# Latent attention: the query products of two tiles in one product, half of a pair's blocks in each tile's step, rows turned four tiles ahead

## What is computed

```python
def _L1_xattn_ref(hidden_q, kv_c, Wq, w_kc_q, w_kc_kv, W_qr, W_kr, Wo):
    q_hk = (hidden_q @ Wq.T).reshape(b, s, H, K)                # H = 16, K = 128
    q_big = jnp.einsum('bshk,hkq->bshq', q_hk, w_kc_q)          # q = 192
    kv_rope = kv_c * cos[None] + _rotate_half(kv_c) * sin[None]
    q_r = jnp.einsum('bshq,hqr->bhsr', q_big, W_qr)             # r = 64
    k_r = jnp.einsum('bld,hdr->bhlr', kv_rope, W_kr)
    scores = jnp.einsum('bhsr,bhlr->bhsl', q_r, k_r)            # l = 257 keys
    attn = jax.nn.softmax(scores, axis=-1)
    ctx_c = jnp.einsum('bhsl,bld->bhsd', attn, kv_rope)
    ctx_lat = jnp.einsum('bhsd,hkd->bshk', ctx_c, w_kc_kv)
    return ctx_lat.reshape(b, s, H * K) @ Wo.T
x = x + _L1_xattn_ref(_layernorm(x, axis=-1), ctx_512, ...)
```

## Time and profile before

| | |
|---|---|
| median of 3 executions | 1148.84 us (1146.88 to 1154.70) |
| the profiled execution | 1154.21 us, of which the profile's span is 1152.4 us |
| PE matmul busy in the span | 1087.5 us, 94% |
| DVE, ACT, POOL busy | 708.1 us (61%), 452.3 us (39%), 301.6 us (26%) |
| L1648, query products of the changed phase | 512 matmuls, 67.8 us busy |
| L1711, output products of that phase, 256 columns | 240 matmuls, 54.4 us busy |

### The profile page before, as it was taken

One profiled execution on the slowest core, in us unless ns is written; L12 is line 12 of the kernel. 1 busy time (PEld: TensorE's weight loads), 2 busy tenths in 40 slices (PEclk: granted clock), 3 DMA queues, 4 the chain that ended last, 5 costly groups with the idle time before them and its releaser, 6 DMA issues. The chain is left out here.

```text
span 1152.4 us, 32210 instructions
## 1 busy us (share of the span) xinstructions
PE 1087.5 (94%) x12466; PEld 830.2 (72%) x12467; DVE 708.1 (61%) x1806; ACT 452.3 (39%) x1329; POOL 301.6 (26%) x390
## 2 busy tenths in 40 slices
PE   7898999999999999999979999999998799899996
PEld 6676878888778768989756766776766588556664
DVE  6898754554646475646547888888885687422221
ACT  2453443434435222221145555555553565222221
POOL 1701523323131200000001221221214535234442
PEclk9899999999999999999989999999999998799998
DMA  8631211111121119000202323333244633312211
GB/s 266 173 89 36 71 46 49 43 39 55 27 55 27 37 35 253 1 0 0 57 1 70 92 75 78 77 84 76 70 139 145 200 77 100 84 30 35 35 27 11
DMA packets 72655, 82.56 MB, mean 72 GB/s; under 512 B 28942, under 2 KB 57263, under 8 KB 72140
## 3 DMA queue, kind: packets, MB, share of 16 engines
q1 hardware_dynamic: 64284, 62.33, 20.4%
q0 software_dynamic: 8304, 19.32, 6.4%
HBM read 64.91 MB, written 18.53 MB: 72 GB/s over the span
## 5 line engine op out<-in xcount | busy, mean ns | idle before, releaser
L1780 ACT ACTIVATE xattn_exps<-xattn_ps_s,xattn_top 128x256 f32<-128x256 f32 x256 | 117.8, 474 | 84.7 <-DVE xattn_top L1844 84.7
L777 PEld LDWEIGHTS attn_ps_q<-attn_xnT,w_b_q 128*128 128x128 f32 x1024 | 120.0, 194 | 12.6 <-issue 12.6
L777 PE MATMUL attn_ps_q<-attn_xnT,w_b_q 128*128 128x128 f32 x1024 | 124.6, 278 | 0.0
L831 PE MATMUL attn_ps_out<-w_b_o,attn_oT 128*128 128x256 f32 x480 | 106.6, 380 | 2.6 <-DVE all_x L1012 1.5
L831 PEld LDWEIGHTS attn_ps_out<-w_b_o,attn_oT 128*128 128x128 f32 x480 | 90.0, 190 | 16.1 <-DVE all_x L1012 2.4
L885 ACT COPY attn_qT<-attn_ps_q 128x512 f32<-128x512 f32 x64 | 38.1, 595 | 148.7 <-PE attn_ps_q L777 148.7
L1851 DVE STREAM_TRANSPOSE xattn_expsT<-xattn_exps 128x1024 f32<-128x1024 f32 x64 | 79.5, 1242 | 26.4 <-ACT xattn_exps L1780 26.3
L1841 DVE TENSOR_REDUCE xattn_raw_top<-xattn_ps_s 128x4 f32<-128x1024 f32 x64 | 77.3, 1208 | 14.7 <-PE xattn_ps_s L1671 14.2
L1648 PEld LDWEIGHTS xattn_ps_o<-xattn_xnT,all_d_a 128*128 128x128 f32 x512 | 61.9, 198 | 17.9 <-ACT xattn_exps L1780 7.2
L1613 POOL TENSOR_TENSOR xattn_ctxT<-xattn_weighed_sum,xattn_inverse 128x256 f32<-128x256 f32 x60 | 41.9, 730 | 125.3 <-DMA xattn_inverse<-xattn_inverse_rows 125.3
L1671 PE MATMUL xattn_ps_s<-all_c,xattn_qT 64*32 64x256 f32 x2048 | 69.8, 382 | 2.8 <-ACT xattn_exps L1780 2.8
(11 more groups left out here) (361 smaller groups left out, 2214.7 us busy)
## 6 DMA issues: line engine op xcount, KB each, us to landing
all_c<-roped_kT SPq DMA_DIRECT2D x32, 256.0 KB, 3.9
xattn_inverse<-xattn_inverse_rows SPq DMA_DIRECT2D x30, 256.0 KB, 4.0
attn_k_raw<-in_ctx SPq DMA_DIRECT2D x64, 64.0 KB, 1.9
roped_kv<-attn_k_kv SPq DMA_DIRECT2D x16, 256.0 KB, 2.1
roped_kT<-attn_k_turned SPq DMA_DIRECT2D x64, 64.0 KB, 1.7
all_c<-roped_kv SPq DMA_DIRECT2D x16, 256.0 KB, 2.9
moe_gate<-in_f_gate SPq DMA_DIRECT2D x8, 512.0 KB, 8.2
moe_up<-in_f_up POOLq DMA_DIRECT2D x8, 512.0 KB, 5.2
```

Of the source, the lines that this page charges most:

```text
L777: last = nc.tensor.matmul(ps_q[g % 2][:, h * P:(h + 1) * P], wq[:, c, head * DH:(head + 1) * DH], xnT[u][:, c, :], start=(c == 0), stop=(c ...
L831: last = nc.tensor.matmul(bank[:, 0:DIM], of_heads[:, h, :, :].rearrange("p b q -> p (b q)"), wo[:, h, :], start=(h == 0), stop=(h == HEAD ...
L1780: nc.scalar.activation(exps[g % 2][:, nkeys * k:nkeys * (k + 1)], ps_s[g % 2][:, nkeys * k:nkeys * (k + 1)], ACT.Exp, bias=top[u][:, n:n + ...
```

## The change

Before, each tile had its own query products. Now the tiles go in pairs (0 and 1, 2 and 3, ...). `xnT` has two buffers of 2 x 256 columns, `qT` two buffers for a pair each. In step t the products of half of the blocks are made for the pair that comes next: for even t, blocks 0 to 3 of tiles t + 2 and t + 3; for odd t, blocks 4 to 7 of tiles t + 1 and t + 2. A product now moves 256 columns. Rows are turned for tile t + 4 instead of t + 2; tiles 0 and 1 are both turned at the start, tile 1 in a score bank. PE and ACT have loops of four steps.

```diff
-        step(i, i % 2, lambda d: 0 <= i + d < tiles)
+        step(i, i % unroll, lambda d: 0 <= i + d < tiles)
...
-    xnT = sb("xnT", [P, KC, P])
-    qT = [sb(f"qT{u}", [P, TB, pairs, SEQ]) for u in range(2)]
+    xnT = [sb(f"xnT{v}", [P, KC, 2 * P]) for v in range(2)]
+    qT = [sb(f"qT{v}", [P, 2, TB, pairs, SEQ]) for v in range(2)]
...
+    def turn_bank(t):
+        return ps_s[1] if isinstance(t, int) and t == 1 else ps_turn
...
             def step(t, u, live):
-                if live(1):
-                    row_normalised(t + 1)
+                if live(3):
+                    row_normalised(t + 3)
                 if live(-2):
                     normalised(t - 2, u)
 
+            row_normalised(2)
+            row_normalised(3)
...
-            def queries(t, part):
+            def queries(t, w, part):
+                pair, half = (w // 2 + 1) % 2, w % 2
                 if part == 0:
-                    pe.wait_ge(s["xnT_ready"], t + 1)
-                if isinstance(t, int) and t == 1:
+                    pe.wait_ge(s["xnT_ready"], min(t + 4, TILES) if isinstance(t, int) else t + 4)
+                if isinstance(t, int) and t == 0:
                     pe.wait_ge(s["last_ready"], 1)
-                wait_count(pe, s["sum_ready"], TB * (t - 2) + 1 + part)
-                for n in range(4):
-                    m = 4 * part + n
+                wait_count(pe, s["sum_ready"], TB * (t - 1) + 1 + part)
+                for n in range(2):
+                    m = 4 * half + 2 * part + n
                     for c in range(KC):
-                        last = nc.tensor.matmul(ps_q[part][:, n * P:(n + 1) * P], a_w[:, c, m * P:(m + 1) * P], xnT[:, c, :],
-                                                start=(c == 0), stop=(c == KC - 1))
+                        last = nc.tensor.matmul(ps_q[part][:, n * 2 * P:(n + 1) * 2 * P], a_w[:, c, m * P:(m + 1) * P],
+                                                xnT[pair][:, c, :], start=(c == 0), stop=(c == KC - 1))
...
-            def step(t, u, live):
-                if live(0):
-                    scores(t, u, 0)
+            def step(t, w, live):
+                u = w % 2
+                if isinstance(t, int) and t == -2:
+                    turn(0)
+                    turn(1)
+                if live(0):
+                    scores(t, w, 0)
...
-                if live(1):
-                    queries(t + 1, 0)
-                if live(0):
-                    scores(t, u, 3)
-                if live(1):
-                    queries(t + 1, 1)
+                if live(2):
+                    queries(t, w, 0)
+                if live(0):
+                    scores(t, w, 3)
+                if live(2):
+                    queries(t, w, 1)
...
-                    pe.wait_ge(s["q_out"], 2 * t + 4)
+                    pe.wait_ge(s["q_out"], min(2 * t + 6, 2 * TILES) if isinstance(t, int) else 2 * t + 6)
...
-                if live(2):
-                    turn(t + 2)
-
-            run_steps(pe, step, -2, TILES, 3, TILES - 3)
+                    last_key(t + 1, (w + 1) % 4)
+                if live(4):
+                    if isinstance(t, int) and t == -2:
+                        pe.wait_ge(s["q_out"], 2)
+                    turn(t + 4)
+
+            run_steps(pe, step, -2, TILES, 3, 10, 4)
...
+            def queries_out(t, w, part):
+                pair, half = (w // 2 + 1) % 2, w % 2
+                m = 4 * half + 2 * part
+                act.wait_ge(s["q_made"], 2 * (t + 2) + part + 1)
+                nc.scalar.copy(qT[pair][:, :, :, m:m + 2, :].rearrange("p a b m q -> p m (a b) q"),
+                               ps_q[part][:, :].rearrange("p (m b q) -> p m b q", m=2, q=SEQ)).then_inc(s["q_out"], 1)
...
-            run_steps(act, step, -2, TILES, 2, TILES - 3)
+            run_steps(act, step, -2, TILES, 2, 9, 4)
```

More of the change, by code:

```diff
@@ L83, in run_steps @@
         for k in range(unroll):
-            step(r + k if k else r, (full_from + k) % 2, lambda d: True)
+            step(r + k if k else r, (full_from + k) % unroll, lambda d: True)
     for i in range(full_from + count, last + 1):
@@ L1617, in row_normalised @@
             def row_normalised(t):
-                wait_count(pool, s["turned"], t)
+                pool.wait_ge(s["turned"], t)
                 nc.gpsimd.tensor_scalar(xn[:, :], x_sb[:, t, :], moments.moments[:, t, 0:1], moments.factors[:, t:t + 1],
@@ L1656, in last_key @@
                         last = nc.tensor.matmul(ps_last[odd][SEQ * b:SEQ * b + SEQ, 0:DIM], last_cols[u][rows, b:b + SEQ],
-                                                qT[u][rows, b, :, :].rearrange("p m q -> p (m q)"), start=True, stop=True)
+                                                qT[w // 2][rows, w % 2, b, :, :].rearrange("p m q -> p (m q)"), start=True, stop=True)
                 last.then_inc(s["last_made"], 1)
@@ L1664, in scores_free, with scores @@
                 wait_count(pe, s["exps_ready"], per_group * (groups * t + g - 1))
-            def scores(t, u, g):
+            def scores(t, w, g):
+                u = w % 2
                 for n in range(2):
@@ L1671, in scores @@
                             last = nc.tensor.matmul(ps_s[g % 2][SEQ * b:SEQ * b + SEQ, 512 * odd + nkeys * n:512 * odd + nkeys * (n + 1)],
[L1672 removed]
+                                                    qT[w // 2][rows, w % 2, b, 2 * g + n, :],
                                                     kT[u][rows, b, :], start=True, stop=True)
@@ L1720, in step @@
                         pe.wait_ge(s["last_ready"], t + 1)
-                    if live(1):
-                        pe.wait_ge(s["xnT_ready"], t + 2)
+                    if live(0):
+                        pe.wait_ge(s["xnT_ready"], min(t + 4, TILES) if isinstance(t, int) else t + 4)
                     wait_count(pe, s["x_ready"], t - 1 if live(0) else t - 2)
@@ L1729, in step @@
                 if live(0):
-                    scores(t, u, 1)
+                    scores(t, w, 1)
                 if live(-1):
@@ L1797, in cols_out, with step @@
                 nc.scalar.copy(last_cols[u][:, :], lastT[:, bass.ds(t * TB, TB + SEQ)]).then_inc(s["cols_ready"], 1)
-            def queries_out(t, u, part):
-                act.wait_ge(s["q_made"], 2 * t + part + 1)
-                nc.scalar.copy(qT[u][:, :, 4 * part:4 * part + 4, :].rearrange("p b m q -> p m b q"),
-                               ps_q[part][:, :].rearrange("p (m b q) -> p m b q", m=4, b=TB)).then_inc(s["q_out"], 1)
-            def step(t, u, live):
+            def queries_out(t, w, part):
[4 more added lines that the diff above has]
+                               ps_q[part][:, :].rearrange("p (m b q) -> p m b q", m=2, q=SEQ)).then_inc(s["q_out"], 1)
+            def step(t, w, live):
+                u = w % 2
+                if isinstance(t, int) and t == -2:
+                    turned_out(0, 0)
+                    turned_out(1, 1)
                 if live(0):
```

25 lines of the change are left out of this document (13 added, 12 removed).

## The result

| | before | after |
|---|---|---|
| median of 15 runs each on one chip, us | 1151.43 (1145.36 to 1156.14) | 1163.47 (1156.97 to 1168.83) |
| ratio, 95% interval | | 1.0117 (1.0095 to 1.0138) |
| profiled execution, span, us | 1154.21, 1152.4 | 1166.15, 1164.3 |
| changed phase, first turn to its last product, us | 289.27 | 299.96 |

The account below looks back on a forecast made before the run. PE was taken to bound the kernel; -4.6 (query products) + 5.7 (start) - 0.7 (turns) + 0.8 (step 14) = +1.2 us, which put on the median of 1148.84 gave 1150.0 us, range 1145 to 1156.

Parts of the forecast that it names:

- What bounds the kernel: Whole kernel: PE, with matmuls in 94% of the span, no other engine above 61%.
- (c): Steps 12 and 13: no turns any more, 0.36 us less each, 0.7 us less together.
- (e): Copies of `qT` and loops of four steps instead of two: no change, 0 us.
- (a): Query products in steps 0 to 13: half the passes, twice as wide; 0.33 us less a step, 4.6 us less.
- The rival, to which I gave 0.08: Query products: the removed weight loads were hidden anyway, so the 4.6 us gain falls away; 1154.6 us, chance 0.08.
- my case: Whole kernel: 1147.5 to 1153 us, with the clock kept or lost in step 14; chance 0.59.
- (b): Start of the phase: additional turn, wider passes and a new chain before the first score; 5.7 us more, bounds 5.3 and 7.5.
- (d): Step 14 without query products: new 3.2 us pause and half clock behind it; 0.8 us more, or 0.55 less if clock stays.
- More clock lost, the rival of 0.13: Pause in step 0 or a late clock rise at the start costs more; 1151.5 to 1155 us, chance 0.13.
- the rival of the other side: ACT's copies of `qT` get slow, 1.27 us instead of 0.58; 1% slower, 1160 us, chance 0.05.
- the last line of the prediction: List of signs that would show the forecast wrong, ending with a pause at the loop's end.

Follow-up runs that it names:

- e1: Kernel before with only PE's loop in the phase made four steps long instead of two; median 1156.03 us, ratio 1.0060.
- e2: Changed kernel with PE's steps written out without a loop, ACT keeping its loop of four; median 1163.01 us, ratio 1.0124.
- e6: Kernel before with PE's steps of the phase written out without a loop; median 1155.63 us, ratio 1.0025.
- e8: Changed kernel run again without edits, on another chip than e1 to e4; median 1165.37 us, ratio 1.0101.
- e3: Changed kernel with three idle products in step 14, run in the pause ahead of the output products; median 1158.74 us, ratio 1.0081.
- e4: Changed kernel with each query product of 256 columns cut into two of 128; median 1169.67 us, ratio 1.0175, two runs.
- f2: Kernel before, unchanged, profiled once more; profiled execution 1151.90 us.
- f3: Kernel before, unchanged, profiled once more as a further sample; profiled execution 1147.30 us.
- f4: Kernel before with PE's steps written out, a second trace of e6; profiled execution 1151.80 us.

## Why the prediction was wrong, point by point

- **What bounds the kernel: right for the middle steps.** PE is busy for 16.82 of 17.00 us there and stands still for 0.18 of a step's 16.98, so a step lasts as long as PE's work in it. After the change the 0.18 us ahead of part 0 is still there, and no engine behind PE took the gain. In step 13 one did, see (c).
- **(e) "Loops of four steps instead of two: 0": wrong, and the step that failed.** I read the cost of a jump back off a loop of two steps, and gave it to a body twice as long, which no row showed. The runs showed a pause of 2.7 to 3.2 us in its place: steps 6 and 7 took 4.23 more instead of 0.66 less, e1 shows 0.6% of the kernel from this edit alone, e2 and e6 show that without the jump the pause is gone. It needed a bound of its own. The pauses that the trace did have give an estimate, for the one jump back: 2.9 for the pause and 1.5 for a stretch of 3 us at half clock, some 4.4 us. Measured against two steps without a pause it was 4.5 in the changed kernel and e8, 5.6 in e3, 7.8 and 8.2 in e1 and e4 with their second pauses; so 4.4 was the least of it.
- **(a) Half the passes: right in kind, 4.6 us was 1.5.** I divided the 16-product block's span by 15 and so spread a fixed cost over the passes. A block of the same size in the second phase has none of it:

```profile
219.82 1.95 PE L777 MATMUL attn_ps_q<-attn_xnT,w_b_q 128*128 128x128 f32 x16
```

  This row of before gives (1.95 - 0.275)/15 = 0.112 us a pass. The block of the earlier trace rows is 2.05, so it carries 0.10 once. The starts of its passes in the trace show where: the second comes 0.213 us behind the first, all others 0.112 apart (wide: 0.320, then 0.216). The record of one lasts 0.275 (wide 0.379), so the records overlap, and what a pass costs is the distance of the starts. The block of eight carries it too: (1.99 - 0.10 - 0.379)/7 = 0.216, the very price of the wide output products. By this a part saves 16 x 0.112 - 8 x 0.216 = 0.06 us; measured were 0.06 and 0.05. Twice the columns cost 1.93 times a narrow pass, and 0.112 - 0.216/2 leaves 4 ns for a load, not 10.

  So the removed loads had been hidden up to those 4 ns. Between the rival's 0 and my 4.6, 1.5 was measured. The rival, to which I gave 0.08, was nearer than my case.
- **(b) The start: right in its steps.** 5.7 was forecast. The table's 4.93 is under the lower bound of 5.3, but it sets a low clock before against a high one after; at the same clock it is 5.9 to 6.1. The 0.2 us that the sum takes off for the clock is shown by no run. In its place the runs showed a start that differs from one execution to the next: in the profiled execution before, the clock was 0.50 from the first turn to 593.4, for 6.3 us; in the six profiles with the change (and in f2, f3 and f4) the turn ran at 1.00, and the clock was 0.50 for 3.4 us, from 0.8 to 1.7 us behind the turn on. The chain between the halves was 1.57 (1.65). The additional turn seems to cost 0.70 where I had 1.15, since both turns took 0.44 and not 0.69.
- **(c) The turns: half right.** 0.73 came off the two steps instead of 1.4, and some 0.2 of it is the width's. Step 12 lost 0.63, step 13 only 0.10: there PE meets POOL's `ctxT` (842.95 and 843.00, above) and waits 0.08 us for DVE's last scores. That is the engine behind PE of which (a) gave the 0.59 to spare; with the turn of step 12 gone too, this is used up one step before step 14.
- **(d) Step 14: the mechanism right, the size not.** A pause of 3.34 us (3.2 forecast) with the clock at 0.50 behind it. I weighed the loss at 1.4 from a stretch of 3 us; the clock stayed low for most of the 6.49 us of the output products (0.56 as the mean of 859.2 to 865.7), 2.87 lost. The step cost 2.55 instead of 0.8, and e3 gave back 3.2.
- **More clock lost, the rival of 0.13:** in step 14 and behind the jump. The +0.56 of step 0 is scatter: it took 13.44 to 15.62 in seven profiles of the step as it was before, and 13.98 to 15.53 in the six with the change.
- **Copies of `qT`, the rival of the other side, did not happen**: 588 ns. The kernel got 1% slower by another road, which stood only in the last line of the prediction, as a pause at the loop's end, with neither price nor chance.
- **The first phase was in no term.** In the profiles with the change the second phase's products start 3 to 4 us later on average; how much that is in the medians isn't shown, and the cause is open, as above.
- **Three sums of the prediction don't come out.** The rival of the lost clock adds up to 1150.0 + 1.5 + 1.8 = 1153.3, and not 1155. The upper bound of (b) is 5.9 + 2 = 7.9, and not 7.5. And 11.5 us are 1.6 times the 7 us that (a) gives at its upper bound, and not more than twice. None of them changes the forecast.

The sum for these two executions, then: -1.5 + 4.9 - 0.5 + 2.55 + 4.4 (the loop's pause, without the width) + 0.7 (step 0, likewise) + 0.15 = 10.7 us in the phase.

## What to carry to other kernels

Price a longer loop body as an unknown of its own: the jump back over a body of twice the instructions isn't in a trace of the short one, and a pause there costs its length and the clock behind it (2.76 us and then 0.62 of the clock here). Before dividing a block's span by its passes, look for a block of the same shape at another place; the fixed part shows in the difference. And when an edit takes filler work out of a step, the waits that it covered come back: idle products in the pause gave 3.2 us of the step back (e3), but here they don't pay for the change. Before reading a difference off one profile of each kernel, see whether the clock was the same in both: the start seemed to cost 4.9 us and costs 6 at the same clock.

## What the runs showed of the hardware

- PE's jump back over four steps (some 2,760 of the trace's instructions) made a pause of 2.7 to 3.2 us in after, e8, e3, e1 and e4, in e1 and e4 with a second one of 1.40 and 2.43; over two steps (some 1,380) there was none, and in the profile of before no packet of `q8 instruction` in the stretch from 681 to 819 us.
- In eight of eight pauses over 1 us put down to "issue" (seven around the jump back, one behind the loop) a packet of 16,384 bytes of `q8 instruction` lands 1.35 to 1.60 us before PE goes on.
- After the same 2.76 us pause in step 0 the granted clock was 1.00 in two executions of the kernel before (before, f3) and fell to 0.50 in a third (f2): 13.44 and 13.45 us for the step, or 15.0.
- A block of 128x128 products behind the small products of the scores carries 0.10 us once, at its first pass; the other passes are 0.112 us apart with 128 columns and 0.216 with 256.
- With edits to one phase, PE's waits for a transfer in another, 550 us earlier, add up to 2.1 to 8.7 us in place of 0 to 1.1, with the same instructions there.
